# A two-layer graph kernel: SyncE's write order, a fourth load buffer, and ScalarE weighing the compacted neighbour rows

## The chip, the cores and the metric

The kernel runs on 1 core of a Trainium2 chip. The metric is the device time of that core in microseconds (us). Before the change the median of 3 runs is 1049.7 us (1049.09 to 1050.65).

## What is computed

The input is x, 8192 rows of 256 floats, and adj, an 8192 x 8192 integer matrix in which about one entry in 4096 is 1, so a row has about two neighbours. Cut to what matters:

```python
h = jnp.maximum(_layernorm(x, axis=-1), 0.0)
x = x + relu(h @ w_self.T + (adj @ h[:, 0])[:, None] * w_neigh.sum(1))   # first layer
h = jnp.maximum(_layernorm(x, axis=-1), 0.0)
Wh = (h @ W).reshape(n, 4, 64)               # 4 heads of 64 columns
e = leaky_relu(sl[:, :, None] + sr.T[None])  # sl, sr: Wh times a_l, a_r, by head
alpha = softmax(where(adj + eye > 0, e, -inf))
x = x + elu(alpha @ Wh)                      # second layer
```

## The kernel before, in words

**The load stage.** The work goes over 64 tiles of 128 rows. SyncE (SP) queues the eight loads of x and then adj, half a tile (128 rows x 4096 integers, 2048 KB) at a time, into a ring of HALVES = 3 buffers in the tile `big`: half-tile number n may be queued once n + 1 - 3 half-tiles have been unloaded (`load`, L254 to L260). TensorE unloads one by eight matmuls that pack the 0/1 entries into numbers (`pack`, L676, matmuls at L685), VectorE searches these for neighbours, and the rest of the first layer and the row table of the second run behind it. Before its first pack TensorE waits for the weights' preparation, which VectorE ends at L350 (semaphore `wa_step`). The raw weights, `wneighT` and the buffers of L348 lie in `big` behind the third load buffer.

The row table `row_dram` holds, for each row, 256 values of Wh and 8 scores. Each node of a tile has up to two "direct" neighbours. Further neighbours of a tile are compacted: each extra edge of the tile sits in one partition, so one more row a partition holds them all, and a 128 x 128 map brings them to their nodes.

**The pair stage.** It goes over 32 pairs of tiles, all buffers being rings of RING2 = 4. For pair t:
- SP's `own_rows` (L885) loads the pair's own rows once `mixed` says that pair t-4 has been mixed; SP's `write` (L893) writes a finished pair. SP's list is `(own_rows, 0), (write, 3)`: in step t it issues own_rows(t), then write(t-3), which waits until VectorE's `take_low` of pair t-3 is done.
- GpSimd (POOL) gathers six sets of rows with indirect DMAs (L912): for each tile of the pair two direct neighbours into G, the compacted ones into E. gather(t) waits for mixed(t-4).
- VectorE (DVE) runs, in step t, in this order: `place`(t) L1012, which waits for own rows and gathered rows; `sum_exps`(t-1) L1043, which waits for ScalarE's exps(t-1); score_direct, invert, add_x(t-3), weights L1051 and L1053, weigh_first and weigh_second(t-1) L1060, `take_low`(t-3) L1097; `score_extra`(t) L1021, which waits for TensorE's scatter(t); `select`(t-1) L1071, which waits for TensorE's spread(t-1); mask, `collapse`(t-1) L1075, which gives the compacted rows' weights `ew`; leaky, `weigh_extra`(t-1) L1081, one operation of 128 x 512 that multiplies E by `ew`; highest, shift(t) L1039.
- TensorE (PE) in step t: scatter(t) L928, spread(t-1) L939, then `mix`(t-1) L952 and L953, sixteen matmuls of 256 columns, which waits for the three weighings and ends in the semaphore `mixed`.
- ScalarE (ACT): list_rows, unfold_maps, `elu_low` L986 and L988 (waits for the mix), `exps` L977 (waits for shift).

The rings' steps are written out by `run` (L228): each engine executes its list of stages in order, each stage with a lag in pairs.

Of the kernel before, what the change touches and what calls it, by code (L numbers as in the profile page):

```python
# [11 lines left out]
ALU = mybir.AluOpType  # L12
ACT = mybir.ActivationFunctionType
AX = mybir.AxisListType

P = 128
EPS = 1e-5
SLOPE = 0.2
RING = 3
RING2 = 4  # L20
HALVES = 3
SLOTS = 16
DIRECT = 2
EXTRA = SLOTS - DIRECT
# [10 lines left out]
def preln_gnn_gat_kernel(nc, x, adj, w_self, w_neigh, w_gat, a_l, a_r, out):  # L35
# [4 lines left out]
    N, D = x.shape  # L40
# [17 lines left out]
    THIRD, FULL = SLOTS, 2 * SLOTS  # L58
    MARKS = FULL + 2
    PAIRS = TILES // 2  # L60
    STAGING = (HALVES + 1) * HALF + 2560
    EMPTY = -0.5

    h0_dram = nc.dram_tensor("h0_table", [N, 1], F32, kind="Internal").ap()
# [3 lines left out]
    with ExitStack() as ctx:  # L68
# [6 lines left out]
        def sem(name):  # L75
            return ctx.enter_context(nc.semaphore(name))
# [14 lines left out]
        def of_big(*shape):  # L91

            width = int(np.prod(shape))
            used[0] += width
            part = bigf[:, used[0] - width:used[0]]
            if len(shape) == 1:
                return part
            if len(shape) == 2:
                return part.rearrange("p (a b) -> p a b", b=shape[1])
            return part.rearrange("p (a b c) -> p a b c", b=shape[1], c=shape[2])  # L100

        at = HALVES * HALF
        w_raw, wn_raw, wneighT = (bigf[:, at + i * DC * D:at + (i + 1) * DC * D].rearrange("p (c d) -> p c d", c=DC)
                                  for i in range(3))
        al_b, ar_b, wa_tmp = (bigf[:, at + (3 * DC + i) * D:at + (3 * DC + i + 1) * D] for i in range(3))
# [103 lines left out]
        def wait_alone(eng, sem, value):  # L209

            if not isinstance(value, int):
                value = eng.to_reg(value)
                eng.wait_ge(consts, 1)
            eng.wait_ge(sem, value)  # L216
# [29 lines left out]
        with nc.Block() as block:  # L246

            @block.sync
            def _(sp):
                for c in range(TILES // XCH):  # L250
                    sp.dma_start(X[:, c * XCH:(c + 1) * XCH, :], x_tiles[:, c * XCH:(c + 1) * XCH, :]
                                 ).then_inc(x_in[c], 16)

                def load(k, r):  # L254
                    for s in range(2):
                        n = 2 * r + s
                        if later_round(k) or n >= HALVES:
                            sp.wait_ge(unloaded, num(k, r) * 2 + s + 1 - HALVES)
                        sp.dma_start(A[n % HALVES], adj[bass.ds(num(k, r) * P, P), s * HALF:(s + 1) * HALF]
                                     ).then_inc(adj_in[n % HALVES], 16)  # L260
                run(sp, (load, 0))
# [328 lines left out]
            def _(pe):  # L590
# [85 lines left out]
                def pack(k, r, s):  # L676
                        t = num(k, r)
                        if s == 0 and not (isinstance(t, int) and t == 0):
                            pe.wait_ge(searched, t)
                        n = 2 * r + s  # L680
                        pe.wait_ge(adj_in[n % HALVES], k * (2 * RING // HALVES * 16) + (n // HALVES + 1) * 16)
                        pe.sem_inc(pack_begun, 1)
                        for i in range(BLOCKS_IN // 2):
                            block_no = s * (BLOCKS_IN // 2) + i
                            last = nc.tensor.matmul(p_pack[:], pack_w[:, block_no, :], low_bytes(n % HALVES)[:, i, :],  # L685
                                                    start=(block_no == 0), stop=(block_no == BLOCKS_IN - 1))
                        last.then_inc(unloaded, 1)
# [34 lines left out]
        with nc.Block() as block:  # L722
# [114 lines left out]
            sem(n) for n in ("maps_ready", "placed", "scattered", "score_step", "shifted"))  # L837
        exp_done, mix_step, weights_spread, edge_step, weighed = (
            sem(n) for n in ("exp_done", "mix_step", "weights_spread", "edge_step", "weighed"))
        mixed, low_step, res_ready, added = (sem(n) for n in ("mixed", "low_step", "res_ready", "added"))  # L840
        num, later_round, run = steps(RING2, PAIRS)

        lists = [sb(f"lists{i}", [P, 2, OWN], U32) for i in range(RING2)]
# [5 lines left out]
        maps = [of_big(2, 2 * P) for _ in range(RING2)]  # L849
        placed_sr, edge_w = ([of_big(2, EXTRA, HEADS) for _ in range(RING2)] for _ in range(2))  # L850
        sc, sc2, pr = ([of_big(2, CAND, HEADS) for _ in range(RING2)] for _ in range(3))
        mx, den, rden = ([of_big(2, HEADS) for _ in range(RING2)] for _ in range(3))
        ew = [p_cnt[:, i * 2 * HEADS:(i + 1) * 2 * HEADS].rearrange("p (a h) -> p a h", a=2) for i in range(RING2)]
        direct_w = [p_pack[:, i * 2 * OWN * HEADS:(i + 1) * 2 * OWN * HEADS].rearrange("p (a j h) -> p a j h", a=2, j=OWN)
                    for i in range(RING2)]
        low = [of_big(2, D) for _ in range(RING2)]
# [24 lines left out]
        with nc.Block() as block:  # L881

            @block.sync
            def _(sp):
                def own_rows(k, r):  # L885
                    t = num(k, r)
                    if later_round(k):

                        sp.wait_ge(mixed, t - RING2 + 1)
                    sp.dma_start(G[r][:, :, 0, :], row_dram[bass.ds(t * (2 * P), 2 * P), :].rearrange("(a p) d -> p a d", p=P)  # L890
                                 ).then_inc(self_in[r], 16)

                def write(k, r):  # L893
                    t = num(k, r)
                    sp.wait_ge(res_ready, t + 1)
                    sp.dma_start(out[bass.ds(t * (2 * P), 2 * P), :].rearrange("(a p) d -> p a d", p=P), res[r]  # L896
                                 ).then_inc(pair_out[r], 16)
                run(sp, (own_rows, 0), (write, 3))
                for r in range(RING2):
                    sp.wait_ge(pair_out[r], 16 * len(range(r, PAIRS, RING2)))  # L900

# [16 lines left out]
            @block.tensor  # L918
            def _(pe):
                def scatter(k, r):  # L920

                    t = num(k, r)
                    pe.wait_ge(placed, t + 1)
                    pe.wait_ge(maps_ready, t + 1)
                    if not (isinstance(t, int) and t == 0):
                        pe.wait_ge(score_step, (t - 1) * SCORE + 2)
                    for a in range(2):
                        last = nc.tensor.matmul(of_pair(p_ext)[:, a], maps[r][:, a, P:2 * P], placed_sr[r][:, a],  # L928
                                                start=True, stop=True)
                    last.then_inc(scattered, 1)  # L930

                def spread(k, r):

                    t = num(k, r)
                    pe.wait_ge(mix_step, (t + 1) * MIX)
                    if not (isinstance(t, int) and t == 0):
                        pe.wait_ge(edge_step, (t - 1) * 2 + 1)
                    for a in range(2):
                        last = nc.tensor.matmul(of_pair(p_spread)[:, a], maps[r][:, a, 0:P], pr[r][:, a, OWN:CAND, :],  # L939
                                                start=True, stop=True)  # L940
                    last.then_inc(weights_spread, 1)

                def mix(k, r):

                    t = num(k, r)
                    pe.wait_ge(weighed, (t + 1) * 3)
                    if later_round(k):
                        pe.wait_ge(added, t - RING2 + 1)
                    for a in range(2):
                        part = p_mix[r][:, a * D:(a + 1) * D]  # L950
                        for j in range(OWN):
                            nc.tensor.matmul(part, ident[:], G[r][:, a, j, 0:D], start=(j == 0), stop=False)  # L952
                        last = nc.tensor.matmul(part, maps[r][:, a, P:2 * P], E[r][:, a, 0:D], start=False, stop=True)  # L953
                    last.then_inc(mixed, 1)
                run(pe, (scatter, 0), (spread, 1), (mix, 1))

            @block.scalar
            def _(act):
# [9 lines left out]
                def unfold_maps(k, r):  # L968
# [3 lines left out]
                        wait_alone(act, mixed, t - RING2 + 1)  # L972
                    nc.scalar.copy(maps[r], maps_all[:, two(k, r), :]).then_inc(maps_ready, 1)

                def exps(k, r):
                    act.wait_ge(shifted, num(k, r) + 1)
                    nc.scalar.activation(pr[r], sc[r], ACT.Exp).then_inc(exp_done, 1)  # L977

                def elu_low(k, r):
# [6 lines left out]
                    nc.scalar.activation(flat, p_mix[r][:], ACT.Exp).then_inc(low_step, 1)  # L986
                    wait_alone(act, low_step, t * 2 + 1)
                    nc.scalar.activation(flat, flat, ACT.Relu, bias=1.0, scale=-1.0).then_inc(low_step, 1)  # L988
                run(act, (list_rows, 0), (unfold_maps, 2), (elu_low, 4), (exps, 2))

            @block.vector
            def _(dve):
# [81 lines left out]
                    dve.wait_ge(edge_step, num(k, r) * 2 + 1)  # L1074
                    nc.vector.tensor_reduce(ew[r], slots_first(edge_w[r]), AX.X, ALU.add).then_inc(edge_step, 1)  # L1075

                def weigh_extra(k, r):
                    dve.wait_ge(edge_step, num(k, r) * 2 + 2)
                    rows_by_head = E[r][:, :, 0:D].rearrange("p a (h k) -> p a h k", h=HEADS)
                    w = ew[r].rearrange("p a (h o) -> p a h o", o=1).broadcast_to([P, 2, HEADS, DK])  # L1080
                    nc.vector.tensor_tensor(rows_by_head, rows_by_head, w, ALU.mult).then_inc(weighed, 1)  # L1081

                def add_x(k, r):

                    t = num(k, r)
# [7 lines left out]
                def take_low(k, r):  # L1093
# [4 lines left out]

                run(dve, (place, 0), (sum_exps, 1), (score_direct, 0), (invert, 1), (add_x, 3), (weights, 1), (weigh_first, 1),
                    (weigh_second, 1), (take_low, 3), (score_extra, 0), (select, 1), (mask, 0), (collapse, 1), (leaky, 0),  # L1100
                    (weigh_extra, 1), (highest, 0), (shift, 0))

# [170 lines left out]
```

## Time and profile before

| | us |
|---|---|
| median of 3 runs | 1049.7 |
| the profiled execution | 1043.53 |
| its span, first to last instruction | 1041.7 |
| PE busy (3025 matmuls) | 720.6 |
| DVE busy | 707.8 |
| ACT busy | 337.8 |
| POOL busy | 397.0 |
| DMA from adj (q1, mostly) | 69.9% of 16 engines' span |

The page cuts the span into 40 slices of 26 us. The DMA row shows tenths of busy share, PEclk the granted clock of TensorE in tenths of full speed:

```profile
PE   1366877877787778687877787786256766766674
DVE  6656676776677766766676677675257777777776
POOL 0032323232323232322323232322277767767660
PEclk9988887888888887988788888888577897789879
DMA  9999999999999999999999999990224444444442
```

The first 27 slices are the load stage, in which DMA is at 9 throughout. The last 11 are the pair stage: DMA at 4, and PE, DVE and POOL each at 6 or 7, none of them full. Busy shares alone don't say what sets its pace.

### The profile page before, as it was taken

Reading aid. Unit: us, or ns where it says so; the run is one execution under the profiler, and the core shown is the slowest. Engines: PE = TensorE matmul, PEld = TensorE weight load, DVE = VectorE, ACT = ScalarE, POOL = GpSimd, SP = SyncE. Lnnn points to the kernel's source line nnn. Section 1 sums busy time; section 2 is a strip of 40 time slices with the busy share of each in tenths; the row PEclk is TensorE's granted clock in tenths of the full one; section 3 lists DMA queues with packets and bytes.
Section 4 is the critical chain, followed back from the end, with each engine's and each line's share of the span. In section 5 each row is a group of like instructions: output and inputs, shape, how many; then the busy total and the mean of one; then the engine's idle time right before and its main releaser. Section 6 shows DMA issues by size and latency. Waiting matters only on the chain. (4 is left out here: it accounts for less than half of the span.)

```text
span 1041.7 us, 13552 instructions
## 1 busy us (share of the span) xinstructions
PE 720.6 (69%) x3025; PEld 478.0 (46%) x3026; DVE 707.8 (68%) x2868; ACT 337.8 (32%) x1481; POOL 397.0 (38%) x458
## 2 busy tenths in 40 slices
PE   1366877877787778687877787786256766766674
PEld 1134544545444444354445444454145555655564
DVE  6656676776677766766676677675257777777776
ACT  1023333333434343434343343335122222232222
POOL 0032323232323232322323232322277767767660
PEclk9988887888888887988788888888577897789879
DMA  9999999999999999999999999990224444444442
GB/s 305 381 423 416 423 422 422 415 420 419 415 408 417 406 408 409 408 417 402 417 407 408 404 409 406 423 385 23 79 70 131 129 120 127 125 126 130 123 122 63
DMA packets 70000, 321.94 MB, mean 309 GB/s; under 512 B 14498, under 2 KB 48721, under 8 KB 53536
## 3 DMA queue, kind: packets, MB, share of 16 engines
q1 hardware_dynamic: 44160, 293.88, 69.9%
q0 software_dynamic: 15360, 17.46, 7.2%
q10 hardware_dynamic: 10400, 9.74, 2.8%
q8 instruction: 26, 0.43, 0.2%
q14 instruction: 54, 0.44, 0.1%
HBM read 312.57 MB, written 17.07 MB: 316 GB/s over the span
## 5 line engine op out<-in xcount | busy, mean ns | idle before, releaser
L685 PE MATMUL p_pack<-big,pack_w 128*128 128x512 fp8e5 x1024 | 316.9, 462 | 150.8 <-DMA big<-in_adj_dram 139.5
L292 POOL DMA_INDIRECT h0g<-h_table,nbr x192 | 191.6, 998 | 476.1 <-ACT nbr L527 390.8
L685 PEld LDWEIGHTS p_pack<-big,pack_w 128*128 128x128 fp8e5 x1024 | 105.4, 108 | 301.2 <-issue 224.3
L912 POOL DMA_INDIRECT big<-row_table,lists x192 | 196.6, 1024 | 97.1 <-issue 54.1
L361 DVE MAX8 tops<-p_pack 128x8 f32<-128x256 f32 x128 | 48.9, 423 | 157.6 <-PE p_pack L685 157.6
L952 PE MATMUL p_u<-big,ident 128*128 128x256 f32 x288 | 94.9, 478 | 62.1 <-DVE big L1081 62.1
L491 ACT ACTIVATE nbr<-keys 128x2 uint32<-128x2 f32 x64 | 13.0, 203 | 366.3 <-DVE keys L396 366.3
L952 PEld LDWEIGHTS p_u<-big,ident 128*128 128x128 f32 x288 | 67.2, 241 | 77.3 <-DVE big L1081 65.3
L650 PE MATMUL p_u<-wselfT,hT 128*128 128x256 f32 x256 | 82.0, 453 | 0.0
L672 PE MATMUL p_row<-w_gat_and_heads,gT 128*128 128x264 f32 x256 | 69.7, 396 | 0.6 <-ACT rows L580 0.6
L650 PEld LDWEIGHTS p_u<-wselfT,hT 128*128 128x128 f32 x256 | 57.6, 249 | 6.5
L1012 DVE TENSOR_TENSOR big<-onehot_all,big 128x112 f32<-128x112 f32 x32 | 8.8, 275 | 76.2 <-DMA big<-row_table 56.6
L1060 DVE TENSOR_TENSOR big<-big,p_pack 128x768 f32<-128x768 f32 x64 | 58.2, 950 | 1.1
L564 ACT ACTIVATE g<-x_rows,nm,rs 128x256 f32<-128x256 f32 x64 | 38.4, 600 | 60.3 <-DVE nm L462 59.8
L365 DVE FIND_INDEX8 found<-tops,p_pack 128x8 uint32<-128x256 f32 x128 | 52.6, 423 | 0.0
L626 PEld LDWEIGHTS p_u<-beyond,mapT 128*128 128x128 f32 x128 | 36.7, 287 | 23.7 <-issue 14.6
L672 PEld LDWEIGHTS p_row<-w_gat_and_heads,gT 128*128 128x128 f32 x256 | 44.7, 195 | 5.6 <-issue 1.2
L952 PE MATMUL p_row<-big,ident 128*128 128x256 f32 x96 | 32.1, 484 | 20.9 <-DVE big L1081 20.9
L977 ACT ACTIVATE big<-big 128x136 f32<-128x136 f32 x32 | 10.1, 316 | 109.8 <-DVE big L1039 109.8
L986 ACT ACTIVATE big<-p_u 128x512 f32<-128x512 f32 x24 | 14.3, 597 | 78.8 <-PE p_u L953 78.8
L535 ACT ACTIVATE h<-x_rows,nmr,rstd 128x256 f32<-128x256 f32 x64 | 37.4, 585 | 0.0
L619 PEld LDWEIGHTS p_u<-extra_all,earlier 128*128 128x128 f32 x128 | 21.6, 190 | 32.0 <-DVE picked L419 26.8
(146 smaller groups left out, 1369.8 us busy)
## 6 DMA issues: line engine op xcount, KB each, us to landing
big<-in_adj_dram SPq DMA_DIRECT2D x128, 2048.0 KB, 12.8
row_table<-rows ACTq DMA_DIRECT2D x64, 132.0 KB, 9.6
big<-row_table SPq DMA_DIRECT2D x32, 264.0 KB, 3.9
x_rows<-in_x_dram SPq DMA_DIRECT2D x8, 1024.0 KB, 12.6
out_dram<-big SPq DMA_DIRECT2D x32, 256.0 KB, 2.2
h0g<-h_table,nbr POOLq DMA_INDIRECT x192, 6.2
big<-row_table,lists POOLq DMA_INDIRECT x192, 2.8
big<-in_L_gnn_w_self_dram ACTq DMA_DIRECT2D x1, 256.0 KB, 4.9
```

The costliest lines, as they stand in the source:

```text
L292: nc.gpsimd.indirect_dma_start(out=h0g[r][:, j:j + 1], out_offset=None, in_=h0_dram[:, :], in_offset=bass.IndirectOffsetOnAxis(ap=nbr[r][: ...
L361: nc.vector.max(tops[r][:, 8 * half:8 * half + 8], p_pack[:, half * WIN:(half + 1) * WIN]).then_inc(search_step, 1)
L365: last = nc.vector.max_index(found[r][:, 8 * half:8 * half + 8], tops[r][:, 8 * half:8 * half + 8], p_pack[:, half * WIN:(half + 1) * WIN])
L535: nc.scalar.activation(h[r][:], x_tile(k, r), ACT.Relu, bias=nmr0[:, bass.ds(t, 1)], scale=rstd0[:, bass.ds(t, 1)]).then_inc(h_ready, 1)
L564: nc.scalar.activation(g[r][:], x_tile(k, r), ACT.Relu, bias=nm1[r][:], scale=rs1[r][:]).then_inc(g_ready, 1)
L626: nc.tensor.matmul(p_edge[:, 0:EXTRA + 1], mapT[r][:], beyond[r][:], start=True, stop=True).then_inc(spread_ready, 1)
L650: nc.tensor.matmul(p_first[:, 0:D], hT[r][:, c * P:(c + 1) * P], wselfT[:, c, :], start=(c == 0), stop=(c == DC - 1))
L672: last = nc.tensor.matmul(p_row[:, 0:ROW], gT[r][:, c * P:(c + 1) * P], wx[:, c, :], start=(c == 0), stop=(c == DC - 1))
L685: last = nc.tensor.matmul(p_pack[:], pack_w[:, block_no, :], low_bytes(n % HALVES)[:, i, :], start=(block_no == 0), stop=(block_no == BLOC ...
L912: nc.gpsimd.indirect_dma_start(out=dst, out_offset=None, in_=row_dram[:, :], in_offset=bass.IndirectOffsetOnAxis(ap=lists[r][:, a, j:j + 1 ...
L952: nc.tensor.matmul(part, ident[:], G[r][:, a, j, 0:D], start=(j == 0), stop=False)
L1060: nc.vector.tensor_tensor(rows_by_head, rows_by_head, w, ALU.mult).then_inc(weighed, 1)
```

## The change

Three things change. The ring of load buffers gets a fourth buffer in the place where the raw weights lie (the size of `big` stays); the fourth half-tile is queued when the weights' preparation is done. SP's `write` gets lag 5 in place of 3. And VectorE's `weigh_extra` goes; ScalarE does it with eight operations of 128 x 64, one for each tile and head, each scaled by a column of `ew`, which moves from PSUM to `big`. They stand in ScalarE's list before `exps`, and TensorE's mix waits for them by a semaphore of their own.

```diff
-HALVES = 3
+HALVES = 4
-    STAGING = (HALVES + 1) * HALF + 2560
+    STAGING = HALVES * HALF + 2560
-        at = HALVES * HALF
+        at = (HALVES - 1) * HALF
@@ SyncE, load stage
-                        n = 2 * r + s
-                        if later_round(k) or n >= HALVES:
-                            sp.wait_ge(unloaded, num(k, r) * 2 + s + 1 - HALVES)
+                        n = 2 * num(k, r) + s
+                        if n >= HALVES:
+                            sp.wait_ge(unloaded, n + 1 - HALVES)
+                        elif n == HALVES - 1:
+
+                            sp.wait_ge(vs_copied, 1)
+                            sp.wait_ge(w_copied, 2)
+                            sp.wait_ge(wa_step, 4 * DC)
@@ buffers of the pair stage
-        mx, den, rden = ([of_big(2, HEADS) for _ in range(RING2)] for _ in range(3))
-        ew = [p_cnt[:, i * 2 * HEADS:(i + 1) * 2 * HEADS].rearrange("p (a h) -> p a h", a=2) for i in range(RING2)]
+        mx, den, rden, ew = ([of_big(2, HEADS) for _ in range(RING2)] for _ in range(4))
@@ SyncE, pair stage
-                run(sp, (own_rows, 0), (write, 3))
+                run(sp, (own_rows, 0), (write, 5))
@@ TensorE, mix
-                    pe.wait_ge(weighed, (t + 1) * 3)
+                    pe.wait_ge(weighed, (t + 1) * 2)
+                    pe.wait_ge(extra_weighed, t + 1)
@@ ScalarE
+                def weigh_extra(k, r):
+                    t = num(k, r)
+                    wait_alone(act, edge_step, (t + 1) * 2)
+                    for a in range(2):
+                        for q in range(HEADS):
+                            cols = E[r][:, a, q * DK:(q + 1) * DK]
+                            last = nc.scalar.activation(cols, cols, ACT.Copy, scale=ew[r][:, a, q:q + 1])
+                    last.then_inc(extra_weighed, 1)
-                run(act, (list_rows, 0), (unfold_maps, 2), (elu_low, 4), (exps, 2))
+                run(act, (list_rows, 0), (unfold_maps, 2), (elu_low, 4), (weigh_extra, 3), (exps, 2))
@@ VectorE
-                def weigh_extra(k, r):
-                    dve.wait_ge(edge_step, num(k, r) * 2 + 2)
-                    rows_by_head = E[r][:, :, 0:D].rearrange("p a (h k) -> p a h k", h=HEADS)
-                    w = ew[r].rearrange("p a (h o) -> p a h o", o=1).broadcast_to([P, 2, HEADS, DK])
-                    nc.vector.tensor_tensor(rows_by_head, rows_by_head, w, ALU.mult).then_inc(weighed, 1)
-                    (weigh_extra, 1), (highest, 0), (shift, 0))
+                    (highest, 0), (shift, 0))
```

## Rows read from the trace of the kernel before

**Rows 1.** Windows: stretch, its length, busy time (instructions) by engine, PEclk, DMA share, GB/s.

```profile
100.00:200.00 100.00, 78.50 (x333) 45.27 (x332) 71.29 (x332) 40.37 (x200) 30.07 (x39) 0.83 1.01 421
...
900.00:1022.00 122.00, 82.65 (x351) 69.35 (x350) 91.20 (x261) 31.79 (x82) 82.26 (x82) 0.85 0.45 123
```

**Rows 2.** Waits, 792 to 1022: us in total, times, longest.

```profile
DVE big L1012 <- DMA big<-row_table: 56.6, 27, 2.8
```

**Rows 3.** Chain that ended last, one step of it: start us, us, what.

```profile
861.52 0.38 SPq L896
...
861.95 4.23 DMA big<-row_table
...
866.30 0.28 DVE big L1012
```

**Rows 4.** Timeline, VectorE, first pairs: start, us, engine, line [idle before <-releaser].

```profile
755.43 0.27 DVE L1012 TENSOR_TENSOR big<-onehot_all,big 128x112 f32<-128x112 f32 x1 [7.89 <-DMA big<-row_table,lists]
...
766.77 0.35 DVE L1075 TENSOR_REDUCE p_cnt<-big 128x8 f32<-128x112 f32 x1
...
778.84 0.27 DVE L1012 TENSOR_TENSOR big<-onehot_all,big 128x112 f32<-128x112 f32 x1 [2.41 <-DMA big<-row_table,lists]
```

**Rows 5.** Timeline, all engines, from one mix's end to the next one's start.

```profile
887.28 0.55 PE L928 MATMUL p_hT<-big 128*128 128x56 f32 x4
...
888.11 0.63 ACT L988 ACTIVATE big<-big 128x512 f32<-128x512 f32 x1
...
888.71 0.35 DVE L1075 TENSOR_REDUCE p_cnt<-big 128x8 f32<-128x112 f32 x1
...
889.91 0.48 PE L952 MATMUL p_u<-big,ident 128*128 128x256 f32 x1 [1.63 <-DVE big L1081]
```

**Rows 6.** Timeline, TensorE, 790 to 1042: starts of mixes (L952) and scatters (L928).

```profile
793.31 1.59 PE L952 MATMUL p_row<-big,ident 128*128 128x256 f32 x6 [2.53 <-DVE big L1081]
...
798.55 0.55 PE L928 MATMUL p_hT<-big 128*128 128x56 f32 x4
...
1000.31 2.93 PE L952 MATMUL p_row<-big,ident 128*128 128x256 f32 x6 [2.61 <-DVE big L1081]
...
1006.83 0.55 PE L928 MATMUL p_hT<-big 128*128 128x56 f32 x4
...
1009.53 2.75 PE L952 MATMUL p_u<-big,ident 128*128 128x256 f32 x6 [1.71 <-DVE big L1081]
...
1014.78 0.55 PE L928 MATMUL p_hT<-big 128*128 128x56 f32 x4
...
1017.41 1.56 PE L952 MATMUL p_u<-big,ident 128*128 128x256 f32 x6 [1.64 <-DVE big L1081]
...
1020.97 0.55 PE L928 MATMUL p_hT<-big 128*128 128x56 f32 x4
```

**Rows 7.** Timeline, ScalarE: a 64-column operation, and two neighbours in the load stage.

```profile
36.50 0.35 ACT L480 ACTIVATE tmp<-tmp,eps 128x64 f32<-128x64 f32 x1 [17.05 <-DVE tmp L333]
...
399.99 0.60 ACT L564 ACTIVATE g<-x_rows,nm,rs 128x256 f32<-128x256 f32 x1 [0.97 <-DVE nm L462]
400.50 0.19 ACT L553 ACTIVATE junk<-h0g 128x2 f32<-128x2 f32 x1
```

**Rows 8.** Start of the load stage: windows, and TensorE's first pack.

```profile
40.00:45.00 5.00, 2.84 (x7) 1.00 (x8) 1.81 (x5) 0.00 (x0) 0.00 (x0) 1.00 0.90 380
45.00:50.00 5.00, 3.28 (x10) 1.01 (x8) 1.58 (x6) 0.00 (x0) 0.10 (x1) 1.00 0.77 269
...
42.16 6.13 PE L685 MATMUL p_pack<-big,pack_w 128*128 128x512 fp8e5 x16 [3.25 <-DVE w_gat_and_heads L350]
```

**Rows 9.** Timeline, the last pair: its place, the collapse of its step, the last mix.

```profile
1019.39 0.28 DVE L1012 TENSOR_TENSOR big<-onehot_all,big 128x112 f32<-128x112 f32 x1 [1.40 <-DMA big<-row_table]
...
1024.00 0.34 DVE L1075 TENSOR_REDUCE p_cnt<-big 128x8 f32<-128x112 f32 x1
...
1031.46 1.56 PE L952 MATMUL p_row<-big,ident 128*128 128x256 f32 x6 [2.15 <-DVE big L1081]
```

More of the change, by code:

```diff
@@ L679, in pack @@
                             pe.wait_ge(searched, t)
-                        n = 2 * r + s
-                        pe.wait_ge(adj_in[n % HALVES], k * (2 * RING // HALVES * 16) + (n // HALVES + 1) * 16)
+                        n = 2 * t + s
+                        pe.wait_ge(adj_in[n % HALVES], (n // HALVES + 1) * 16)
                         pe.sem_inc(pack_begun, 1)
@@ L839, in preln_gnn_gat_kernel @@
             sem(n) for n in ("exp_done", "mix_step", "weights_spread", "edge_step", "weighed"))
-        mixed, low_step, res_ready, added = (sem(n) for n in ("mixed", "low_step", "res_ready", "added"))
+        extra_weighed, mixed, low_step, res_ready, added = (sem(n) for n in ("extra_weighed", "mixed", "low_step", "res_ready", "added"))
         num, later_round, run = steps(RING2, PAIRS)
```

## The prediction

> **What bounds the kernel now.** I read the 40 slices first: they show two stages with different limits, so each is read by itself. In the load stage the windows give a DMA share of 1.01 at 421 GB/s [rows 1]; TensorE and VectorE are at 0.79 and 0.71. Only a more continuous stream of loads can shorten it. In the pair stage the DMA share is 0.45 and no engine is full: in 122 us VectorE is busy 91.20, TensorE 82.65, POOL 82.26 [rows 1]. There a loop of dependences sets the pace, and the waits and the chain name it. VectorE waits at `place` for the pair's own rows in all 27 pairs of the stretch, 56.6 us in total [rows 2]. The chain shows why: SP issues `write` at 861.52, right behind it `own_rows` at 861.95, the rows come after 4.23 us, and `place` starts at 866.30 [rows 3]. own_rows(t+1) stands behind write(t-3), which waits for `take_low` in VectorE's step t. So a step is VectorE's work from place to take_low, then SP, then a whole transfer. From the collapse at 766.77 + 0.35 = 767.12 [rows 4] to that of step 31 at 1024.34 [rows 9] there are 30 steps: 8.574 us each.
>
> The first pairs, whose own rows come early, show the next bound. Their `place` waits for the gathered rows, and the three steps from 755.43 to 778.84 take 7.80 each [rows 4]: POOL's pace.
>
> There is a third loop, through TensorE, and the change touches it. mix(t-2) must end before scatter(t) and spread(t-1); select and collapse(t-1) need these; weigh_extra(t-1) needs the collapse, and mix(t-1) needs weigh_extra(t-1). I split it at the start of a scatter. Where VectorE waits for TensorE, the loop can be measured: scatter at 887.28, collapse until 888.71 + 0.35 = 889.06, mix at 889.91 [rows 5], so 2.63 from scatter to mix, of which 0.85 lies after the collapse. The pair of mixes at 1009.53 and 1017.41 gives the same: 7.88 less the 5.25 from mix to scatter is 2.63 [rows 6]. The rest is the mix's length, m, from its start to the next scatter. It has no single value, as TensorE's clock changes between 1.2 and 2.4 GHz. Over 27 mixes (first 793.31 to 798.55, last 1017.41 to 1020.97 [rows 6]) ten take 3.56, thirteen 5.0 to 5.5, four 6.1 to 6.6 (such as 1000.31 to 1006.83 [rows 6]); the mean is 4.79. This loop is thus at 2.63 + 4.79 = 7.42 on average, 1.15 below the present pace, and hidden.
>
> **The parts of the change.**
>
> *Fourth load buffer.* The stream of loads has one dip: 380 GB/s from 40 to 45 us and 269 from 45 to 50 [rows 8], against 421 later. Missing are 5 x 41 + 5 x 152 = 965 KB, or 2.3 us at 421 GB/s. Three half-tiles are queued and the fourth waits for the first unload, at half of the packs' 6.13 us behind 42.16, about 45.2 [rows 8]. The new fourth waits for L350 instead, which releases TensorE at the same 42.16 [rows 8]; it is queued some 3 us earlier, and the fifth at 45.2. The dip should go: -2.2 us, with bounds 0 and -3. After that the DMA engines are already at 1.01 [rows 1], and a deeper queue gives nothing more.
>
> *write at lag 5.* write(t-5) waits for take_low(t-5), done in VectorE's step t-2, so own_rows(t+1) goes out as soon as mix(t-3) has ended, about a step and a half before place(t+1). That covers its 4.2 us. add_x's wait for the write of four pairs earlier is met a step or more ahead. Alone this would take the pace from 8.57 to the next bound: the larger, pair by pair, of 7.80 for POOL and 2.63 + m for TensorE.
>
> *weigh_extra to ScalarE.* VectorE loses an operation of 0.68 that holds its path for about 0.6. It isn't its own work that bounds VectorE, so this buys nothing. What counts is that the eight operations stand between collapse and mix, in TensorE's loop. The only 64-column operation with an operand from a column of SBUF took 0.35, and an operation starts 0.09 before its forerunner's end (399.99 + 0.60 against 400.50) [rows 7]. So 0.26 apiece and the last 0.35: 7 x 0.26 + 0.35 = 2.17, with 0.03 before and 0.05 behind for the handovers 2.25 from collapse to mix where there were 0.85: +1.40. Bounds: a two-column operation takes 0.19 [rows 7], which would make 7 x 0.10 + 0.19 + 0.08 = 0.97, +0.12; with no overlap at all 8 x 0.35 + 0.08 gives +2.03. The 0.35 has the right width and operand, so I take it. ScalarE has just ended elu_low then (888.11 + 0.63 = 888.74 against the collapse's 889.06 [rows 5]), so it starts at once.
>
> Beside that row stands a rule. The Trainium skill, "ScalarE: Activation LUTs", section "What ACT_TABLE_LOAD costs", gives 186 ns + 0.833 ns a column, 93 ns more for each column operand and an overlap of 93 ns; as an estimate that is 0.33 a piece and 2.01 for the eight, 0.16 less than by the row, or some 5 us less over 30 steps. The same page's section "Rules for kernel authors" says that multiplications belong on VectorE, which speaks against this move.
>
> `exps` now stands behind the eight, too: it ends 0.03 + 2.17 + 0.32 - 0.09 = 2.43 after the collapse instead of about 1.8. VectorE's sum_exps waits for it, and its path from there to the next collapse is about 4.8, together 7.2. That is below 7.80, so it doesn't bind.
>
> *The new loop.* 2.63 + 1.40 + m = 4.03 + m: 7.59 after a fast mix, 9.28 after one of 5.25, 10.6 after one of 6.6. Only the first is below POOL's 7.80. The question is m. TensorE's wait before each mix grows from the 1.64 to 1.71 of the loop's own pace [rows 6] to about 3.05 in every pair. Over the 27 mixes m goes with that wait: six with 1.6 to 1.8 average 4.40 (three of them fast); nine with 2.4 to 2.9 average 4.79 (four of them fast; the one at 1000.31, with 2.61 before it, was among the slowest [rows 6]); eight with 3.2 to 3.5 average 5.32 (none fast). Between the last two classes I take 4.95, with ends 4.4 and 5.5 (the mean of all that weren't fast).
>
> **The sum.** The pace becomes 4.03 + 4.95 = 8.98. TensorE's loop starts in step 1, so the collapse of step 31 comes at 767.12 + 30 x 8.98 = 1036.5 in place of 1024.34: +12.2. The tail from there to the last mix at 1031.46 [rows 9] gets 1.40 for the last weighing and about 1.1 for the later exps and spread: +2.5, if the last mixes stay fast as now, and up to 1.7 more if one doesn't. The load stage gives -2.2. Together +12.5. The profiled execution took 1043.53 us, 1.8 more than its span and 6 less than the median of the runs; it would take 1056.0. The difference is carried over to the median: 1049.7 + 12.5 = 1062.2.
>
> So the removed stall is real, but the loop that comes next has been lengthened beyond it: of the 22 us that POOL's pace would give (rival A) nothing is left.
>
> **The rivals.**
>
> *A, POOL's pace, the other sign.* If nearly all mixes run fast (m up to 3.77), the own rows' transfer is off the chain and POOL decides: place(31) at 755.43 + 31 x 7.80 = 997.2 instead of 1019.39 [rows 4, 9], -22.2; with -2.2 and +2.5 the time is 1027.8. For it: the fast mixes are ten of 27 now, and every pair would look alike. Against it: no mix of the eight with a wait above 3.2 was fast. 10%.
>
> *B, the same loop with a better clock.* With m = 4.40, as at the short waits, the pace is 8.43, the collapse of step 31 at 1020.0, the sum -4.3 - 2.2 + 2.5 = -4.0: 1045.7. The point from which the change loses is m = 4.54. 14%.
>
> *C, cheap operations.* If the column operand costs nothing and the eight take about 1.3, the loop is 3.2 + 4.6 = 7.8 to 8.0, so -17 to -20 and a time of about 1033. The row of 0.35 speaks against it. 5%.
>
> *D, a colder clock.* If no mix is fast any more, m is 5.5, the pace 9.53, the step's collapse 28.7 later: 1079. The eight long waits are for it, the nine middling ones against it. 10%.
>
> *E, the order doesn't take own_rows off the chain,* as if something else held SP. Then the pace is at least 8.57 in every pair, after a mix of 3.56 too, which adds about 0.3 a pair: 1071. Nothing in the trace speaks for it. 3%.
>
> **How the numbers follow.** The forecast has 58%. The range takes B whole and most of D's side: 1040 to 1076; A, C and D's upper half are left out, two in ten. About 0.2% (2 us) is what a measurement can tell from no change. Faster: A, C, most of B, and a little of the forecast's lower side, 27%. Same 8%, from the edges of B and the forecast. Slower: the rest, 65%.
>
> **What would show it.** VectorE's place no longer waits for row_table and SP's own_rows goes out right after a mix: the first step of the argument. The eight ScalarE operations at 0.33 to 0.35, 0.26 apart, and TensorE's longest wait in the pair stage naming ScalarE, about 3.0 a pair: the second. Steps of 7.6 after mixes of 3.56 and 9.3 after mixes of 5.25: the third. The mean of m near 4.95 and the granted clock of the stage at or below the 0.85 of before: the fourth, and the weakest. In the load stage no window below 400 GB/s between 40 and 50 us, and everything behind it 2 us earlier. The prediction is wrong if the mixes run mostly at 2.4 GHz, or if the eight take much less than 2 us.

## The result, and the profile after

The kernel after takes 1096.8 us (median of 3 runs, 1095.45 to 1100.86) where the kernel before took 1049.7: 4.56% slower, the ratio 1.0456 with a 95% interval of 1.0411 to 1.0501. The sign was forecast, the size was not: 1062.2 with a range up to 1076. The profiled execution took 1095.45 us, 51.9 more than that of before.

The page's slices after, of 27 us each (rows as in the profile of before):

```profile
PE   1358788667786778778777776851676776776775
DVE  6657677776777667676766766643655555555553
PEclk9988888898888988788888899875866666666666
DMA  9999999999999999999999999403444444444330
```

Before, the granted clock in the pair stage moved between 7 and 9 tenths; now it stands at 6 in each of the last eleven slices. VectorE is down to 5. Over 200 us of the stage (columns as in [rows 1]):

```profile
800.00:1000.00 200.00, 141.45 (x471) 115.49 (x470) 117.04 (x335) 82.93 (x280) 123.18 (x118) 0.67 0.42 107
```

A granted clock of 0.67, against 0.85 in [rows 1].

The timeline of one step, all engines; it answers to [rows 3] and [rows 5]:

```profile
872.18 0.55 PE L932 MATMUL p_hT<-big 128*128 128x56 f32 x4
...
872.38 0.37 SPq L894 DMA_DIRECT2D big<-row_table  x1
...
872.79 0.47 SPq L900 DMA_DIRECT2D out_dram<-big  x1
...
873.61 0.34 DVE L1089 TENSOR_REDUCE big<-big 128x8 f32<-128x112 f32 x1
...
873.98 2.02 ACT L986 ACTIVATE big<-big 128x64 f32<-128x64 f32 x8 [0.34 <-DVE big L1089]
...
874.84 0.27 DVE L1026 TENSOR_TENSOR big<-onehot_all,big 128x112 f32<-128x112 f32 x1
...
876.10 2.90 PE L957 MATMUL p_row<-big,ident 128*128 128x256 f32 x6 [2.93 <-issue]
```

The own rows (L894) go out at the end of a mix, ahead of the write, and `place` (L1026) no longer waits. The collapse (L1089) ends at 873.95, ScalarE starts 0.03 later and works for 2.02, and the mix begins at 876.10. TensorE has idled for 2.93 us. The profile itself writes "issue" there and names ScalarE only for the first four mixes; that the mix waits for ScalarE follows from the program and from its start, 0.10 after ScalarE's end at 876.00. From scatter to mix it is 876.10 - 872.18 = 3.92.

TensorE's timeline over the stage; it answers to [rows 6]:

```profile
865.86 2.90 PE L957 MATMUL p_u<-big,ident 128*128 128x256 f32 x6 [2.93 <-issue]
...
876.10 2.90 PE L957 MATMUL p_row<-big,ident 128*128 128x256 f32 x6 [2.93 <-issue]
878.80 1.06 PE L958 MATMUL p_row<-big 128*128 128x256 f32 x2
879.65 2.50 PE L957 MATMUL p_row<-big,ident 128*128 128x256 f32 x6
881.99 0.59 PE L958 MATMUL p_row<-big 128*128 128x256 f32 x2
882.42 0.55 PE L932 MATMUL p_hT<-big 128*128 128x56 f32 x4
...
1070.66 2.90 PE L957 MATMUL p_u<-big,ident 128*128 128x256 f32 x6 [2.93 <-issue]
```

From mix to mix it is 10.24 us here. The 27 steps from the mix at 794.23 to the one at 1070.66 all lie between 10.22 and 10.25, and every mix in them takes 6.29 to 6.32 to the next scatter: six matmuls at 2.90 (1.2 GHz), two at 1.06, six more in 2.50 during which the clock rises, and the last two at 0.59 (2.4 GHz). In the kernel before, steps lay between 7.2 and 9.2, and a mix and the next could differ by 2.5 us. 3.92 + 6.32 = 10.24 is the whole step: TensorE's loop alone, with a clock that changes at the same point of every step.

Waits of the stage, 792 to 1070 (columns as in [rows 2]):

```profile
DVE big L1035 <- PE p_hT L932: 76.3, 27, 2.9
...
PE p_u L957 <- issue: 58.5, 20, 2.9
...
POOL big L916 <- PE p_u L958: 43.0, 18, 2.4
...
DVE big L1026 <- DMA big<-row_table,lists: 1.0, 1, 1.0
```

VectorE (at score_extra) and POOL both wait for TensorE now; the 56.6 us of [rows 2] are gone. The 58.5 us are TensorE's idle time ahead of the mixes into `p_u`.

The start of the load stage, which answers to [rows 8]:

```profile
40.00:45.00 5.00, 3.01 (x8) 1.10 (x9) 1.68 (x4) 0.00 (x0) 0.00 (x0) 1.00 1.00 425
45.00:50.00 5.00, 3.05 (x13) 1.12 (x12) 2.34 (x11) 0.00 (x0) 0.10 (x1) 1.00 1.00 427
```

The dip is filled, and the pair stage's first own_rows goes out at 742.64 instead of 744.36, 1.7 us earlier.

### The profile page after: what moved, and what is told of

The parts are those of the page before. It is cut to its first block and busy times, and to the rows that moved or that the text cites. A ratio compares the mean times of both kernels' runs of the same rounds, so it can differ in the third digit from the quotient of the medians.

```text
span 1093.6 us, 13781 instructions
## 1 busy us (share of the span) xinstructions
PE 754.3 (69%) x3025; PEld 501.0 (46%) x3026; DVE 695.7 (64%) x2836; ACT 398.9 (36%) x1737; POOL 401.5 (37%) x458
## 5 line engine op out<-in xcount | busy, mean ns | idle before, releaser
L690 PE MATMUL p_pack<-big,pack_w 128*128 128x512 fp8e5 x1024 | 310.6, 455 | 159.5 <-DMA big<-in_adj_dram 143.7
L916 POOL DMA_INDIRECT big<-row_table,lists x192 | 200.9, 1047 | 134.1 <-issue 50.6
L957 PE MATMUL p_u<-big,ident 128*128 128x256 f32 x288 | 125.8, 603 | 71.1 <-issue 61.5
L957 PEld LDWEIGHTS p_u<-big,ident 128*128 128x128 f32 x288 | 90.0, 322 | 94.3 <-issue 73.6
L655 PE MATMUL p_u<-wselfT,hT 128*128 128x256 f32 x256 | 77.2, 431 | 0.0
L986 ACT ACTIVATE big<-big 128x64 f32<-128x64 f32 x256 | 64.6, 334 | 17.9 <-DVE big L1089 17.9
L1035 DVE TENSOR_TENSOR big<-p_hT,big 128x112 f32<-128x112 f32 x32 | 8.8, 274 | 80.0 <-PE p_hT L932 80.0
L957 PE MATMUL p_row<-big,ident 128*128 128x256 f32 x96 | 43.4, 621 | 23.5 <-issue 20.5
L957 PEld LDWEIGHTS p_row<-big,ident 128*128 128x128 f32 x96 | 30.8, 331 | 31.6 <-issue 24.3
L958 PE MATMUL p_u<-big 128*128 128x256 f32 x96 | 39.3, 501 | 0.0
```

The lines of the kernel that those rows point to most:

```text
L655: nc.tensor.matmul(p_first[:, 0:D], hT[r][:, c * P:(c + 1) * P], wselfT[:, c, :], start=(c == 0), stop=(c == DC - 1))
L916: nc.gpsimd.indirect_dma_start(out=dst, out_offset=None, in_=row_dram[:, :], in_offset=bass.IndirectOffsetOnAxis(ap=lists[r][:, a, j:j + 1 ...
L986: last = nc.scalar.activation(cols, cols, ACT.Copy, scale=ew[r][:, a, q:q + 1])
```

## The experiments

Two theories were put against each other. **Additive**: a step is 3.92 plus a mix whose length is a property of the clock, irregular or fixed, so what is added between collapse and mix adds to the step. **Locking**: when TensorE's loop alone sets the pace, the steps are all alike, and the point at which its clock falls and rises takes hold of them; the step is then one of a few values, and the mix's length gives way. Each experiment's runs are compared with runs of the kernel before on the same chip, whose median was 1044.7 to 1046.8 there; two experiments that ran on different chips are better compared by their ratios than by their times.

### The other two changes without ScalarE (e1)

```diff
-                    pe.wait_ge(weighed, (t + 1) * 2)
-                    pe.wait_ge(extra_weighed, t + 1)
+                    pe.wait_ge(weighed, (t + 1) * 3)
@@ weigh_extra is back in VectorE's list, as before; ew stays in SBUF
```

> The kernel after with weigh_extra back on VectorE; write at lag 5, the fourth buffer and ew outside PSUM stay. Additive theory (the new pace is 2.63 + m, m irregular with mean about 4.4 to 4.8): 7.8 to 7.9 a pair because POOL's 7.80 is the floor, so about 1.7 us from the load stage and 20 to 22 from the pairs: 1026 to 1032 us. Locking theory (once nothing but TensorE's loop sets the pace, steps settle on a fixed one, as the 10.24 us of the kernel after): a loop of 2.63 + m can't be 10.24 even when every matmul is at 1.2 GHz (m about 7.1), so it gives the same here. Rival, the lag itself is what costs (writes collide with own rows): pace above 9 and above 1060 us.

Measured: 1032.3 us (1029.1 to 1033.3), ratio 0.986 (0.981 to 0.991). The lag is no cost. The loss is all in the weighing: 1096.8 against this. But the steps are 8.3 to 8.4 (mean over all 31 steps, from collapse to collapse, 8.27), not 7.8. POOL sets them, and its gathers are longer than in the first pairs; e8 below takes this up.

### ScalarE's weighing alone (e2)

```diff
-HALVES = 4
+HALVES = 3
@@ the load stage as in the kernel before
-                run(sp, (own_rows, 0), (write, 5))
+                run(sp, (own_rows, 0), (write, 3))
```

> The kernel before with only the weighing moved to ScalarE (three buffers, write at lag 3; ew outside PSUM). Own rows are on the chain again. If the loss is TensorE's loop with its clock, nothing changes against the kernel after but the 1.7 us of the load stage: steps of 10.24 us, 1097 to 1100 us. If the order of SP has a part in it, or the locking needs it, the pace is 8.6 to 9.3 and the time 1050 to 1072 us.

Measured: 1098.0 us (1096.8 to 1099.4), ratio 1.049 (1.044 to 1.054). Its steps are 10.24 from the fifth on and its mixes 6.31 or 6.32. SP's order has no part in the loss. It isn't a test of the lock from another start, though: its first mix begins 4.0 us later than in the kernel after, but its first four mixes (5.93, 3.53, 5.21, 6.29) and the steps between them (9.90, 7.50, 9.18) are those of the kernel after to the hundredth, so the whole course was only shifted.

### TensorE kept busy while it waits (e4)

```diff
+                def busy(k, r):
+                    for i in range(6):
+                        nc.tensor.matmul(p_cnt[:], pack_w[:, i, :], pack_w[:, 0:4, :], start=True, stop=True)
-                run(pe, (scatter, 0), (spread, 1), (mix, 1))
+                run(pe, (scatter, 0), (spread, 1), (busy, 1), (mix, 1))
```

> The kernel after, with six matmuls of 128x512 fp8 put between spread and mix, into a PSUM bank that nothing reads, so that TensorE works in the 2.93 us in which it waits for ScalarE. If the clock is what makes a mix 6.32 us long, the mixes fall to 3.6, the loop to 3.92 + 3.6 = 7.5, POOL's 7.80 decides and the time is about 1022 to 1030 us, with a granted clock near 1.0 in the pair stage. If the mixes are long for another reason (ScalarE in the same SBUF rows, contention), they stay, and TensorE's added work makes it no faster: 1095 to 1110 us.

Measured: 1027.3 us (1026.1 to 1027.7), ratio 0.982 (0.977 to 0.986). Windows and a step of TensorE's timeline in this kernel:

```profile
800.00:1000.00 200.00, 153.88 (x750) 117.45 (x750) 148.47 (x425) 103.46 (x349) 153.15 (x149) 0.96 0.49 135
```

```profile
880.49 1.53 PE L957 MATMUL p_u<-big,ident 128*128 128x256 f32 x6 [1.87 <-issue]
...
884.02 0.55 PE L932 MATMUL p_hT<-big 128*128 128x56 f32 x4
...
884.85 1.46 PE L962 MATMUL p_cnt<-pack_w 128*128 128x512 fp8e5 x6
888.04 1.53 PE L957 MATMUL p_row<-big,ident 128*128 128x256 f32 x6 [1.74 <-issue]
```

With six matmuls whose result nobody reads, 1.46 us of them a step, the granted clock goes from 0.67 to 0.96, 23 of 30 mixes take 3.53 instead of 6.32, and the kernel is 69 us faster than the one after (67 by the ratios), with ScalarE's eight operations where they were. So the clock is what made the mixes long, and giving TensorE work in its idle time is enough to raise it. ScalarE's operations cost little by themselves: with a fast mix TensorE's loop is 3.92 + 3.53 = 7.45, below POOL's 7.8. That the clock simply falls as the idle time grows is not shown, and the runs below speak against it: from 880 to 1000 us it was 0.80 with 2.45 of idle time before each mix (e7), 0.66 with 2.69 (e11), 0.67 with 2.93 (the kernel after) and 0.74 with 3.67 (e5).

### A longer way from collapse to mix (e5)

```diff
+                            for c in range(2 if q < 2 else 1):
+                                w = DK // 2 if q < 2 else DK
-                            cols = E[r][:, a, q * DK:(q + 1) * DK]
+                                cols = E[r][:, a, q * DK + c * w:q * DK + (c + 1) * w]
```

> The kernel after, with ScalarE's weighing in twelve operations (four of the eight cut in two halves of 32 columns), which lengthens the way from collapse to mix by some 0.7 to 0.8 us. Additive theory with m fixed at 6.32: steps of 11.0 us and 1115 to 1122 us. Locking theory: the steps are held at 10.24 us by TensorE's clock, a later start of the mix meets the rise of the clock earlier in the mix, m falls by the 0.75 to about 5.6, and steps and time stay as they are: 10.24 and 1095 to 1100 us.

Measured: 1098.4 us (1097.1 to 1099.0), ratio 1.050 (1.044 to 1.055). TensorE's timeline here:

```profile
880.07 1.82 PE L957 MATMUL p_row<-big,ident 128*128 128x256 f32 x6 [3.67 <-issue]
...
885.29 0.55 PE L932 MATMUL p_hT<-big 128*128 128x56 f32 x4
...
889.95 2.90 PE L957 MATMUL p_u<-big,ident 128*128 128x256 f32 x6 [3.67 <-issue]
...
895.89 0.55 PE L932 MATMUL p_hT<-big 128*128 128x56 f32 x4
...
900.56 1.82 PE L957 MATMUL p_u<-big,ident 128*128 128x256 f32 x6 [3.67 <-issue]
```

TensorE idles for 3.67 instead of 2.93, 0.74 more a pair, and the kernel is not slower than the one after by anything that can be measured (1.6 us; 30 times 0.74 would be 22). In the traces the 30 steps from the first mix take 306.2 us against 303.0, and the whole difference lies in the first three steps, before the pattern begins. The steps are then 9.88 and 10.61 in turn, mean 10.24; the mixes 5.22 and 5.94, mean 5.58, which is the 6.32 less the 0.74. The additive theory, with m fixed at 6.32, falls.

### A shorter way: six operations and seven (e7, e11)

```diff
-                        for q in range(HEADS):
+                        for q in range(HEADS - 1):
@@ e11: range(HEADS - a), seven operations
```

> The kernel after with ScalarE weighing only the first three heads of each tile, six operations (the fourth head's compacted rows stay unweighed, a part of the computation is left out). The way from collapse to mix is 0.48 shorter. Additive theory with m at 6.32: 9.76 a pair, about 1083 us. Locking theory: the mix starts 0.5 us of TensorE's fixed pattern earlier, has that much more of the slow clock, m rises to about 6.8 and the steps stay at 10.24: 1095 to 1100 us.

Measured: 1042.5 us (1037.2 to 1046.5, 10 runs), ratio 0.996 (0.994 to 0.999). Both expectations missed. After 12 steps without a pattern, 7.0 to 10.0 us long, the steps are 8.66 and 8.41 in turn, mean 8.53, the mixes 5.22 and 4.97:

```profile
874.09 1.60 PE L957 MATMUL p_u<-big,ident 128*128 128x256 f32 x6 [2.45 <-issue]
...
879.30 0.55 PE L932 MATMUL p_hT<-big 128*128 128x56 f32 x4
...
882.74 2.90 PE L957 MATMUL p_u<-big,ident 128*128 128x256 f32 x6 [2.45 <-issue]
...
887.71 0.55 PE L932 MATMUL p_hT<-big 128*128 128x56 f32 x4
...
891.16 1.61 PE L957 MATMUL p_row<-big,ident 128*128 128x256 f32 x6 [2.46 <-issue]
```

It is a repeating pattern again, but another one. So the lock has more than one value, and I then asked for the middle:

> The kernel after with seven of the eight operations (the last head of the second tile stays unweighed, a part of the computation is left out). Six gave steps of 8.66 and 8.41 in turn (mean 8.53), eight gave 10.24, twelve a mean of 10.24. If TensorE's clock holds the steps at a few paces, seven has one of the two, 8.53 or 10.24 (1038 to 1046 or 1095 to 1100 us), and nothing between. If the loss grows evenly with the time between collapse and mix, seven lies half way: a mean step of 9.4, about 1068 us.

Measured: 1096.6 us (1083.9 to 1098.2), ratio 1.044 (1.039 to 1.049), with steps of 10.24 and mixes of 6.56: the mix is longer by the 0.24 that the missing operation saves.

```profile
880.25 2.90 PE L957 MATMUL p_row<-big,ident 128*128 128x256 f32 x6 [2.69 <-issue]
...
886.80 0.55 PE L932 MATMUL p_hT<-big 128*128 128x56 f32 x4
...
890.48 2.90 PE L957 MATMUL p_u<-big,ident 128*128 128x256 f32 x6 [2.69 <-issue]
```

It doesn't start there. Its first mixes take 6.24, 6.37, 6.44, 6.48 and 6.52 and its first steps 9.97, 10.10 and 10.17, each nearer to 6.56 and 10.24 than the one before: the loop is drawn to that step. Between six and seven operations 0.24 us of ScalarE's work moves the kernel by 54 us; between seven and twelve 1 us moves it by 2 (6 by the ratios, whose intervals overlap). That is the locking theory, in the form that it took after e7. One of the four runs came 12 us lower; no trace of it was kept, and that it reached the pattern later is a guess.

### The mix ahead of its wait (e6)

```diff
-                    pe.wait_ge(extra_weighed, t + 1)
+                        if a == 0:
+                            pe.wait_ge(extra_weighed, t + 1)
                         last = nc.tensor.matmul(part, maps[r][:, a, P:2 * P], E[r][:, a, 0:D], start=False, stop=True)
```

> The kernel after, in which the mix no longer waits for ScalarE's weighing at its start: the first tile's six matmuls of direct rows go ahead and the wait stands before the seventh. If the eight operations cost because they stand between collapse and all of the mix, and TensorE idles for 2.9 us, this takes most of both away: the six run in the idle time (1.6 to 2.9 us), the loop is 3.92 + m less some 1.5 to 2.7, steps near POOL's 7.8 to 8.2, 1025 to 1045 us. If the lock is stronger than that and holds 10.24 us, 1095 us or more.

Measured: 1024.2 us (1023.6 to 1026.4), ratio 0.980 (0.975 to 0.984); steps of 7.9 on average, granted clock 0.89 from 800 to 900 us and 0.94 from 900 to 1000. One mix of it, TensorE's timeline:

```profile
820.79 1.56 PE L956 MATMUL p_row<-big,ident 128*128 128x256 f32 x6 [0.97 <-DVE big L1075]
824.28 0.70 PE L959 MATMUL p_row<-big 128*128 128x256 f32 x2 [1.93 <-ACT big L987]
```

The compacted rows are only read by the seventh and eighth matmul instructions of a tile, so the first six can run while ScalarE works. Moving one wait undoes the whole loss and makes the changed kernel faster than the one before.

### Where the weights lie (e8)

```diff
-        mx, den, rden, ew = ([of_big(2, HEADS) for _ in range(RING2)] for _ in range(4))
+        mx, den, rden = ([of_big(2, HEADS) for _ in range(RING2)] for _ in range(3))
+        ew = [p_cnt[:, i * 2 * HEADS:(i + 1) * 2 * HEADS].rearrange("p (a h) -> p a h", a=2) for i in range(RING2)]
@@ on top of e1
```

> e1_two_others with ew back in PSUM. In e1 steps of 8.35 us followed POOL, whose gathers took 1.33 us beside weigh_extra and 1.14 beside take_low instead of 1.00. In the kernel before the same weigh_extra reads its weights from PSUM and only take_low lengthens a gather. If two operands in SBUF are what lengthens a gather, the one beside weigh_extra returns to 1.00, the step to about 8.0 and the time to 7 to 10 us below e1's, about 1023 us. If it is the mere overlap with a long VectorE operation, nothing changes: 1029 to 1033 us.

Measured: 1024.6 us (1022.5 to 1025.7), ratio 0.979 (0.974 to 0.983), 8 us below e1. The timeline of VectorE's weighing and the gathers beside it, in e1 and then in e8:

```profile
897.76 0.69 DVE L1085 TENSOR_TENSOR big<-big 128x512 f32<-128x512 f32 x1
897.99 1.33 POOL L916 DMA_INDIRECT big<-row_table,lists  x1 [0.30 <-issue]
...
904.42 0.68 DVE L1101 TENSOR_TENSOR big<-big 128x512 f32<-128x512 f32 x1
904.84 1.14 POOL L916 DMA_INDIRECT big<-row_table,lists  x1 [0.31 <-issue]
```

```profile
837.99 0.67 DVE L1086 TENSOR_TENSOR big<-big,p_cnt 128x512 f32<-128x512 f32 x1
838.21 1.00 POOL L917 DMA_INDIRECT big<-row_table,lists  x1 [0.31 <-issue]
...
898.30 1.00 POOL L917 DMA_INDIRECT big<-row_table,lists  x1 [0.30 <-issue]
898.47 0.68 DVE L1102 TENSOR_TENSOR big<-big 128x512 f32<-128x512 f32 x1
```

What counts is the moment at which the gather starts. If a VectorE operation of 512 columns with both operands in SBUF is running then, the gather takes longer by about the time that this operation still has to run, less 0.13 us: 0.46 left gives 1.33 and 0.26 left gives 1.14 in the first view. The longest in e8 is 1.51; its two exceptions, at 1.00, are gathers that start 0.03 to 0.04 us behind such an operation. If the same operation starts while the gather is under way, the gather keeps its 1.00 (898.30). With an operand in PSUM (838.21) it keeps 1.00 even when the operation is running at its start, in all 12 such cases of e8. So it is the second SBUF operand, and not the mere overlap. Over most of the stage a gather took 1084 ns on average in e1 and 1019 in e8, six of them 0.39 us a step, and the steps went from 8.27 to 7.95. The Trainium skill, "VectorE: DVE Perf Modes", section "Two Vector instructions with no wait between them", says that an operation's second SBUF input is read through an interface shared with GpSimd; these rows agree with it.

### SP's lag and the fourth buffer, each alone (e3, e10)

```diff
@@ e3, on the kernel before
-                run(sp, (own_rows, 0), (write, 3))
+                run(sp, (own_rows, 0), (write, 5))
@@ e10, on the kernel before: HALVES = 4 and the load stage as in the kernel after
```

> The kernel before with write at lag 5 and nothing else. The own rows' transfer leaves the chain; ew stays in PSUM, so the pace should be that of e8, 7.95 a pair, and the time 2 us above e8's for lack of the fourth buffer: some 17 to 20 us below before. If the fourth buffer carried part of e8's gain, it is less than 15 us below.

> The kernel before with the fourth load buffer and nothing else. By the traces one of the 16 DMA engines works on alone at the end of the loads, so a deeper queue lets the others run ahead and only the dip at 45 us goes: 1.7 us less, close to what this measurement can resolve, and no other change. If the deeper queue helps the stream at large, 4 us or more.

Measured: e3 1029.1 us (1026.5 to 1030.7), ratio 0.984 (0.982 to 0.986), 17 us less, steps of 7.95, at the lower end of what was expected; it is 4.5 us above e8 where I had 2. e10 1042.2 us (1036.6 to 1045.1, 12 runs), ratio 0.996 (0.995 to 0.998): 4.0 us less, with an interval of 2 to 6. That leaves out the 1.7 that I expected and reaches the 4 of its rival. The trace gives less: the first own_rows at 742.12, 2.2 earlier than before, and a pair stage of the same length (257.3 us from the first mix to the thirty-first, 257.2 before). So 2.2 us are shown, all of them in the load stage, and whether the other 2 us are real stays open. The windows at the end of e10's loads:

```profile
690.00:698.00 8.00, 5.63 (x25) 3.74 (x24) 4.90 (x19) 3.08 (x13) 3.11 (x4) 0.79 0.43 168
698.00:704.00 6.00, 3.11 (x16) 1.74 (x15) 5.37 (x27) 3.25 (x17) 1.11 (x2) 0.99 0.06 21
```

A share of 0.06 is one engine of 16. In the kernel before the share is 1.04 and 0.57 in the same windows. The packets in the traces say the same: in e10 the loads' queue has one packet at a time under way from 694 us on, in the kernel before from 703. The deeper queue lets 15 engines finish some 8 us early, and TensorE still waits for the last one, which is done only some 2 us earlier: the last half-tile's packing begins at 704.06 instead of 706.34.

### The best version (e9)

On e8: the mix's wait before its seventh matmul instruction, and the six idle-time matmuls of e4 (`ew` in the bank `p_pack`, to leave `p_cnt` to them).

> write at lag 5, four load buffers, weighing on VectorE with ew in PSUM, the mix waiting for it only before its seventh matmul, and six fp8 matmuls of 512 columns between spread and mix. TensorE's loop is then some 6 us and POOL alone sets the pace: steps of 7.9 to 8.0 us, 1018 to 1026 us. If TensorE's clock still decides some pairs it is no faster than e8: 1023 us or more.

Measured: 1025.0 us (1023.9 to 1025.9), ratio 0.979 (0.975 to 0.984). That lies in both expected ranges; the trace tells them apart. The granted clock is 1.00 from 800 to 1000 us and the steps are even at 8.0, yet it is no faster than e8 or e6. At this pace nothing is left to gain from TensorE; POOL's six gathers are the step, with no more than 0.3 us of idle time ahead of any of them in that stretch. They take 1036 ns on average here against e8's 1019, because with even steps `take_low` runs at the start of a gather in nearly every step. The versions e6, e8 and e9, some 2.1% below before, can't be told apart.

## Why the prediction was wrong, point by point

- **The own rows' transfer leaves the chain.** Right: place has no wait for the own rows left, own_rows goes out as a mix ends, and e3 alone gives 17 us.
- **The fourth buffer, -2.2.** Right by the traces: -1.7 in that of after, -2.2 in e10's, and the dip is filled; e10's median of -4.0 leaves open whether there is more. Where the traces show nothing more, it is for a reason that I hadn't seen: the windows' mean share hides that one engine is the last.
- **ScalarE's eight operations, 2.17 and +1.40.** Nearly right: 2.02, and 3.92 from scatter to mix where I had 4.03. The estimate from the figures of the Trainium skill, "ScalarE: Activation LUTs", section "What ACT_TABLE_LOAD costs", 2.01, was nearer than mine from the single row of 0.35.
- **VectorE's own path doesn't bind.** Right: it waits 76.3 us for TensorE.
- **The form of the loop, 4.03 + m.** Right, and it shows in the first pairs: after a mix of 3.53 the step is 7.50, after one of 5.21 it is 9.18.
- **The mix's length, 4.95.** This is the step that failed: 6.32. I had read mixes as draws whose mean depends on the wait before them, and interpolated between classes with waits of 2.65 and 3.4. Both ends were taken from a kernel in which steps differ from one another, since own rows and TensorE's loop took turns at the bound. When one loop remains every step is the same (or two take turns), and the clock meets it at the same point each time: not a mean over all cases, but one case, repeated. e5, e7 and e11 show it: 3.67 of idle time gives mixes of 5.58 on average, 2.93 gives 6.32 and 2.69 gives 6.56, opposite to the trend of the classes, and 2.45 gives 5.09, which fits no trend. The row at 1000.31, 2.61 of idle time and a mix of 6.52, was a better guide than the mean of its class, 4.79; that can be said only now, as the same class had four fast mixes. The error is (6.32 - 4.95) x 30 = 41 us, less 3 for the 3.92. Of the 39 us by which the profiled execution passed its forecast, 34 lie between the first mix and the thirty-first (303.0 us against 30 x 8.98 = 269.4); most of the rest is the last two mixes, which took 6.32 and 6.71 where the kernel before had 3.56 and 3.71.
- **The rivals.** A (POOL's pace, 21.9 us less than before) is what e6, e8 and e9 reach with 21.8 to 22.6 less, and e4 with 17.4; it needed TensorE at work in its idle time, the later wait, or the weighing left with VectorE and its weights in PSUM. D (a colder clock) had the right direction but m = 5.5, the mean of all mixes that weren't fast, where it should have asked which single length repeats. I gave it 10%. The range ended at 1076 because both its ends rested on means (m = 4.4 and 5.5). The loop's own bounds, 7.6 and 10.6, stood in the prediction, and the 10.24 lies within them.

Left open is why eight operations settle at 10.24 and six at 8.53, and whether the kernel after could be held in another pattern by its start alone. No run here gave it another start: e2's course was the same, 4.0 us later.

## What to carry to other kernels

When a change leaves TensorE's loop as the only bound, don't take the mean of its matmul times from a trace in which steps vary. Expect one pattern to repeat, and let the range reach from the loop with the shortest of those times to the loop with the longest. An operation moved to an idle engine isn't free if TensorE has to wait behind it; look first whether the wait can stand later, ahead of the matmul that reads the result (e6). And a few matmuls of no use in TensorE's wait can be worth far more than they cost (e4).

## What the runs showed of the hardware

- With TensorE's loop alone in charge the steps are equal to within 0.03 us over 27 pairs, and a change of 0.24 to 0.74 us inside the step is taken back to the hundredth by the mix: 6.56, 6.32 and a mean of 5.58 at seven, eight and twelve operations, all with a mean step of 10.24. With six it isn't: 8.53.
- 0.24 us of work on another engine moved this kernel by 54 us.
- The granted clock of the stage was 0.67 with an idle time of 2.93 before each mix, and 0.96 with 1.46 us of fp8 matmuls put into it. It didn't follow the idle time alone: 0.80, 0.66 and 0.74 at 2.45, 2.69 and 3.67 us.
- A GpSimd gather that started while a 512-column VectorE operation with two operands in SBUF was running took 1.12 to 1.51 us instead of 1.00 where 0.24 us or more of the operation were left. With one operand in PSUM it took 0.99 to 1.01.
- One DMA engine of 16 ended the loads some 8 us behind the others once the queue was four deep.
